# In the first unit of a 1-core FFN and convolution kernel, VectorE makes two of three low parts of the weights and the row statistics behind its reads of a step's last two products instead of in front of them

## The reference, cut to what matters

```python
x = L0_attn_u                                            # (1, 2048, 512) float32
x = x + 0.5 * _L0_ffn_ref(_layernorm(x), ...)            # 6-bit weights, dequantised; one 512x512 linear layer
x = x + _L0_attn_ref(_layernorm(x), ...)                 # S4: convolution along the 512 features + D*u
x = x + 0.5 * _L0_ffn_ref(_layernorm(x), ...)
x = x + 0.5 * _L1_ffn_ref(_layernorm(x), W_gate, W_up, W_down)   # first use
x = x + _L1_attn_ref(_layernorm(x), ...)
x = x + 0.5 * _L1_ffn_ref(_layernorm(x), W_gate, W_up, W_down)   # second use

def _L1_ffn_ref(x, W_gate, W_up, W_down):                # W_gate, W_up: (1376, 512), W_down: (512, 1376)
    up = xt @ W_up.T
    gate = jax.nn.silu(xt @ W_gate.T)
    return gate * up @ W_down.T
```

## Time and profile before

| | |
|---|---|
| median of 3 runs | 926.05 us (925.15 to 927.67) |
| the profiled execution: its time, its span | 925.5 us, 923.7 us |
| TensorE busy | 887.5 us (96%) |
| VectorE busy | 620.8 us (67%) |
| ScalarE, GpSimd busy | 314.3 us (34%), 368.5 us (40%) |
| HBM traffic | 160 GB/s over the span |
| mean granted TensorE clock | 0.990 |
| unit 0, first M1 to the end of its last M3 | about 193 to 337 us |

### The profile page before, as it was taken

How to read it: one execution, slowest core, us unless ns; L and a number is a source line. 1 busy time by engine, 2 the same in 40 slices (tenths; PEclk the granted TensorE clock), 3 DMA queues, 4 the chain that set the end, 5 groups by cost and what they waited for, 6 DMA issues and landing times.

```text
span 923.7 us, 11734 instructions
## 1 busy us (share of the span) xinstructions
PE 887.5 (96%) x4116; PEld 723.7 (78%) x4116; DVE 620.8 (67%) x1057; ACT 314.3 (34%) x517; POOL 368.5 (40%) x729
## 2 busy tenths in 40 slices
PE   8989998789999999999999999999999999999998
PEld 4777887567777787888888887888888778888876
DVE  7778776698888879655566786555566875545452
ACT  4423444634433434222314361222233522222121
POOL 4965366842232336332324453232343542222211
PEclk7989999999999999999999999999999999999999
DMA  8200000036766695565554656546455757666345
GB/s 323 95 1 1 1 1 1 1 131 236 272 222 225 237 339 170 152 203 153 157 169 139 204 166 188 172 137 183 140 190 160 219 145 233 201 205 205 126 141 178
DMA packets 41310, 148.27 MB, mean 161 GB/s; under 512 B 3490, under 2 KB 3746, under 8 KB 39844
## 3 DMA queue, kind: packets, MB, share of 16 engines
q0 software_dynamic: 29040, 100.93, 35.9%
q1 hardware_dynamic: 12212, 46.59, 13.8%
HBM read 117.36 MB, written 30.15 MB: 160 GB/s over the span
## 4 chain that ended last, share of the span: by engine, by line
PE 75%; DVE 14%; POOL 4%; issue 3%; DMA 2%; ACT 2%; SPq 0%; DVEq 0%; ACTq 0%; POOLq 0%
PE front L1408 14%; PE front L1410 13%; PE front L1409 13%; PE acc L1362 6%; PE acc L1364 6%; PE acc L1363 6%; PE front L454 3%; PE acc L1299 3%; PE acc L1298 3%; PE acc L1297 3%; DVE hidden_lo L1208 3%; DVE weight_operands L583 2%; DVE snapshots L1168 2%; DVE gate_up L1168 1%; DMA down_weights<-saved_down 1%
## 5 line engine op out<-in xcount | busy, mean ns | idle before, releaser
L1408 PE MATMUL front<-row_operands_hi,weight_operands 128*128 128x512 f32 x616 | 242.7, 394 | 9.0 <-DVE snapshots L1168 8.1
L1410 PE MATMUL front<-row_operands_hi,weight_operands 128*128 128x512 f32 x616 | 240.0, 390 | 0.0
L1409 PE MATMUL front<-row_operands_lo,weight_operands 128*128 128x512 f32 x616 | 239.9, 389 | 0.0
L1408 PEld LDWEIGHTS front<-row_operands_hi,weight_operands 128*128 128x128 f32 x616 | 115.6, 188 | 37.9 <-issue 10.6
L1362 PE MATMUL acc<-down_weights,hidden_hi 128*128 128x512 f32 x352 | 140.1, 398 | 3.8 <-DMA down_weights<-saved_down 1.9
L1168 DVE TENSOR_TENSOR snapshots<-front,snapshots 128x512 f32<-128x512 f32 x132 | 91.0, 689 | 78.1 <-PE front L1410 76.9
L1364 PE MATMUL acc<-down_weights,hidden_lo 128*128 128x512 f32 x352 | 137.3, 390 | 0.0
L1363 PE MATMUL acc<-down_weights,hidden_hi 128*128 128x512 f32 x352 | 137.2, 390 | 0.0
L1410 PEld LDWEIGHTS front<-row_operands_hi,weight_operands 128*128 128x128 f32 x616 | 115.6, 188 | 24.5
L1409 PEld LDWEIGHTS front<-row_operands_lo,weight_operands 128*128 128x128 f32 x616 | 115.8, 188 | 23.1
L801 POOL DMA_DIRECT2D weight_operands<-saved_weights x66 | 48.6, 737 | 184.4 <-PE front L1410 179.2
(11 more groups left out here) (169 smaller groups left out, 1358.8 us busy)
## 6 DMA issues: line engine op xcount, KB each, us to landing
weight_operands<-saved_weights POOLq DMA_DIRECT2D x33, 1280.0 KB, 6.4
down_weights<-saved_down POOLq DMA_DIRECT2D x77, 512.0 KB, 4.0
saved_weights<-weight_operands SPq DMA_DIRECT2D x11, 1792.0 KB, 8.3
weight_operands<-saved_weights POOLq DMA_DIRECT2D x33, 512.0 KB, 4.2
raw_weights<-wgu SPq DMA_DIRECT2D x11, 512.0 KB, 4.4
saved_down<-down_weights SPq DMA_DIRECT2D x11, 512.0 KB, 3.3
x_rows<-x_in SPq DMA_DIRECT2D x3, 1024.0 KB, 12.1
out<-x_rows SPq DMA_DIRECT2D x3, 1024.0 KB, 5.3
```

The source lines that it names most:

```text
L1408: T.matmul(o, wh, xh, start=(j == 0), stop=False)
L1409: T.matmul(o, wh, xl, start=False, stop=False)
L1410: last = T.matmul(o, wl, xh, start=False, stop=(j == 1))
```

## The change: what it does

`weight_lows` gets a list of the parts that it makes. In step k of unit 0 VectorE's queue now has low0 where all three stood; low1 and low2 stand behind C12 and in front of `hidden_lo`; the statistics stand behind `hidden_lo`, at the end of the step. Units 1 to 3 keep their order (they make no low parts, and their statistics stay in place). No instruction is added or taken away, no wait of another engine is changed, and SP's `save_weights(k + 1)`, which waits for all three low parts, now waits for a later instruction. The low parts for step 0, made ahead of the unit, stay together.

```diff
-        def weight_lows(dve, k):
+        def weight_lows(dve, k, parts):
             dve.wait_ge(w_step, 4 * k + 4)
-            for i, (first, last) in enumerate(((A22, A12 + 1), (S2, S3 + 1), (S4, S4 + 1))):
+            for i in parts:
+                first, last = ((A22, A12 + 1), (S2, S3 + 1), (S4, S4 + 1))[i]
                 dve.wait_ge(w_hi, 3 * k + i + 1)
...
                     middle_sums_c(k)
                     if k + 1 < FT:
-                        weight_lows(dve, k + 1)
+                        weight_lows(dve, k + 1, (0,))
...
-                    for n in STATS_OF_STEP[u][f]:
-                        stats_step(dve, n)
-                        aggregate_step(dve, n)
+                    if u:
+                        for n in STATS_OF_STEP[u][f]:
+                            stats_step(dve, n)
+                            aggregate_step(dve, n)
                     if 1 <= f <= EMBEDDED[u]:
                         xt_lo_step(dve, embedded_item(u, f - 1))
                     first_hidden(k)
                     second_gate(k)
+
+                    if k + 1 < FT:
+                        weight_lows(dve, k + 1, (1, 2))
                     hidden_lo(q, g0)
+                    if u == 0:
+                        for n in STATS_OF_STEP[u][f]:
+                            stats_step(dve, n)
+                            aggregate_step(dve, n)
```

More of the change, by code:

```diff
@@ L1161, in _ @@
                 if n == PRE - 3:
-                    weight_lows(dve, 0)
+                    weight_lows(dve, 0, range(3))
             def add(k, product, read, out, other):
```

## The result

| | before | after |
|---|---|---|
| median | 925.07 us (6 runs, 924.43 to 927.67) | 930.67 us (6 runs, 928.67 to 931.18) |
| ratio to before, 95% interval | | 1.0048 (1.0035 to 1.006) |
| profiled span | 923.7 us | 928.2 us |
| a step of unit 0, M1 to M1 | 13.25 us | 13.63 us |
| unit 0, first matmul of M1 of step 0 to last of M3 of step 10 | 142.8 us | 145.4 us |

The interval stands for 3.2 to 5.6 us, middle 4.4. The forecast was 929.2, slower.

What follows compares the result with a forecast made beforehand. It took a closed VectorE and TensorE chain, 13.25 us a step, to bound unit 0. −1.0 + 8 × 0.45 − 0.07 + 0.66 made +3.2 us, 929.2 on the median's scale; range 918 to 932, likeliest case 926.5 to 931.5.

Steps and rivals of the forecast that it cites:

- M1's wait goes: Unit 0's steps: C21 needs only M4, so M1 follows M3 without a gap; 1.0 us a step is taken away.
- `second_hidden` falls on low2, 1.12 us: Behind C12 in unit 0: GpSimd's product blocks VectorE's low2, which ends at 3.00 instead of 1.88 us; bounds 0 and 1.29.
- M5 0.7 late, M6 0.7 late; period 13.72: TensorE in unit 0 waits for low2 and C11, 1.4 us together; a step lasts 13.72 against 13.25 us.
- my +3.2 for unit 0: Whole change: −1.0 in step 0, 0.45 in each of eight steps, −0.07 in the first of these, +0.66 in step 9.
- −1.0 in step 0: Unit 0's first step, where TensorE waited longest: M5 of step 1 comes at 209.8 instead of 210.8 us.
- The save, priced 0: SP's save of the low parts waits for low2 and goes some 3.4 us later, at no cost.
- My last rival: Unit 0: the later save delays the next `load_raw`, up to 1 us a step, +8 on top, 937 us; chance 0.06.
- The first rival (918.4): Unit 0: GpSimd takes no turn at VectorE's cost, period 12.60 us, 7.7 us saved in all; chance 0.21.

Runs made afterwards that it cites:

- e3: The changed kernel with GpSimd's `second_hidden` of unit 0 also waiting for `hidden_lo` of its own step: 918.84 us, ratio 0.9929 to before.
- e1: Against the kernel before, only unit 0's statistics move behind `hidden_lo`; the three low parts stay in front of C21: 918.96 us, ratio 0.9926.
- e2: Against the kernel before, only low1 and low2 move behind C12; the statistics stay in front of C21: 925.54 us, ratio 0.9997.
- e4: Against the kernel before, low1 and low2 behind C12, statistics in front of C21, `second_hidden` held until after `hidden_lo`: 916.62 us, ratio 0.9912.
- e8: The changed kernel with GpSimd making the `second_hidden` product twice in unit 0, the second into the next slot: 938.78 us, one run.

## Why the prediction was right

The sign, the place and the mechanism hold, and the time lies in the range. By its own steps:

- *M1's wait goes.* Shown: the waits of after have no row for `snapshots`.
- *`second_hidden` falls on low2, 1.12 us.* low2 took 1.53 instead of 0.41: 1.12. The start was forecast 1.43 behind C12 and is 247.18 − 245.75 = 1.43. e3 takes this turn away and nothing else, and 1.10 us of the step go with it.
- *M5 0.7 late, M6 0.7 late; period 13.72.* The stalls are there (0.41 and 0.39 in TensorE's rows beside the weight loads' own), and the period is 13.63. C11 starts 4.34 behind C12, forecast 4.35. From M5 to the next C12 it is 8.54 (250.84 to 259.38), forecast 8.53. The difference lies between C11 and M5: C11 ends at 250.78 and M5 starts 0.06 behind it, where I had taken 0.15 from C21 and M1. This is what made my +3.2 for unit 0 a measured +2.6: −1.0 in step 0 as forecast, +0.38 in each of eight steps instead of 0.45, and +0.6 in step 9.
- *The statistics' and low parts' shares.* e1 and e2 part them: the statistics alone bring a step to 12.44, the low parts alone to 12.98, both together to 13.63. Each alone makes a step shorter than before. Of what GpSimd takes, 0.74 us a step reaches TensorE with the low parts alone (12.98 against the 12.24 of e4). Together with the statistics the 1.15 us in front of C11 are used up, and 1.10 of the 1.12 reach it (13.63 against 12.53).
- *The save, priced 0.* This step failed, though it cost little. I had the save go "some 3.4 later" and expected it to be quicker there. In the middle steps it was quicker (6.2 us in the median of the unit, 8.3 before), and nothing waited for it. The last save took 10.4 us, it landed 6.5 us later than before (341.47 against 334.97, of which 2.9 are the unit's own delay), and a down load was queued behind it. My last rival had the save become a bound for `load_raw`, the wrong customer. By the two traces it is 1.7 us of the 4.5, and these I had at 0. The +3.2 was too small by these, and too large by the 0.6 above. That the two errors work against each other is luck, and so is part of the nearness of 929.2 to 930.67: I had started from a median of 926.05, which with six runs is 925.07. The change itself, 3.2 forecast, lies at the lower end of the measured 3.2 to 5.6.
- *The first rival (918.4)* did not happen, but e3, where its condition is made true by a wait, gave 918.84 and a step of 12.53 against its 12.60. Its unit is 8.0 us shorter than before, against the rival's 7.7; the passes then lose 2.6, which the rival did not have, and the unit's earlier start hides part of it in the trace.

## What to carry to other kernels

Before an instruction is moved into an idle stretch of one engine, look what another engine runs in that stretch: an idle time in which a neighbour has its turn is not free. Here 256 columns cost 1.53 us in the new place instead of 0.41, and one wait on GpSimd, which had time, took 1.10 us off a step. When a store moves with its producer, follow the queue that waits for the store to its end, and the last round most of all, since it meets the loads of the next phase.

## What the runs showed of the hardware

- VectorE's and GpSimd's turns. GpSimd won over a VectorE instruction whose row starts 0.04 us after its own (low2) and, in the trace of before, over one whose row starts 0.13 us ahead of it: `hidden_lo` at 354.72, alone 0.69 us, stood still for GpSimd's two 256-column instructions.

```profile
354.72 2.13 DVE L1208 TENSOR_TENSOR hidden_lo<-second_hidden,hidden_hi 128x512 fp32r<-128x512 f32 x1
```

```profile
354.85 1.45 POOL L532 TENSOR_TENSOR row_operands_lo<-pair_sums,row_operands_hi 128x256 fp32r<-128x256 f32 x2
```

- In e8, with two 512-column instructions of GpSimd, VectorE did get its turn between the two; with the two of 256 above it did not. Why is open.
- The Trainium skill, "SBUF — State Buffer", section "SBUF: two separate sides", says that only a VectorE instruction with two SBUF inputs (or a two-port mode) is held by GpSimd. The traces agree: `bn_stats`, with one input, took 0.68 us beside `second_hidden` in e1 and e3, and C11, with one input in PSUM, 0.69.
